# Graph network, last layer: one block for normalisation, weights, neighbours' products and the first sums

## The reference

```python
h = jnp.maximum(_layernorm(x, axis=-1), 0.0)
mask = (adj > 0).astype(x.dtype)
deg = jnp.sum(mask, axis=1, keepdims=True)
agg = mask @ h / jnp.maximum(deg, 1.0)
self_f = h @ W_self + b_self
nb_f = agg @ W_nb + b_nb
combined = jnp.concatenate([self_f, nb_f], axis=-1)
x = x + jax.nn.relu(combined @ W_comb + b_comb)
```

## Time and profile before

| | us |
|---|---|
| median of three runs | 2232.77 |
| the profiled execution, its own time | 2228.39 |
| its span, first to last instruction | 2226.7 |
| outside the span | 1.7 |
| the last layer, from the first DVE instruction of block one (2004.06) to the last output's DMA | 222.6 |
| of it: from 2004.06 to the first matmul of `sums(1)` (2065.77) | 61.7 |
| of it: from there to the end of the last matmul | 156.8 |

### The profile page before, as it was taken

One profiled execution on the slowest core, in us unless ns is written; L12 is line 12 of the kernel. 1 busy time (PEld: TensorE's weight loads), 2 busy tenths in 40 slices (PEclk: granted clock), 3 DMA queues, 4 the chain that ended last, 5 costly groups with the idle time before them and its releaser, 6 DMA issues. The chain is left out here.

```text
span 2226.7 us, 58732 instructions
## 1 busy us (share of the span) xinstructions
PE 1983.5 (89%) x23674; PEld 1553.7 (70%) x23674; DVE 1892.4 (85%) x4169; ACT 1614.1 (72%) x1924; POOL 926.3 (42%) x932
## 2 busy tenths in 40 slices
PE   5758999999986899999695999999999999886999
PEld 4548999999985788888553666666666666555544
DVE  5587999999997899987786999999999999985222
ACT  4557999999985776542444999999999999885100
POOL 0020000000006344454144888888888888860000
PEclk9958999999997899999796999999999999998999
DMA  9797211211201356778374122111121111101222
GB/s 313 293 360 291 98 67 56 99 65 63 95 12 41 85 136 154 165 169 175 70 159 134 61 70 70 70 54 53 70 70 70 65 41 70 39 2 53 81 81 70
DMA packets 173436, 233.32 MB, mean 105 GB/s; under 512 B 110113, under 2 KB 140865, under 8 KB 169839
## 3 DMA queue, kind: packets, MB, share of 16 engines
q1 hardware_dynamic: 148766, 201.87, 29.8%
q10 hardware_dynamic: 24400, 27.70, 3.8%
HBM read 156.67 MB, written 47.30 MB: 92 GB/s over the span
## 5 line engine op out<-in xcount | busy, mean ns | idle before, releaser
L1956 DVE CUSTOM_DVE_ANT_0 h_S<-h_ps,h_off 128x832 f32<-128x832 f32 x832 | 800.5, 1020 | 14.9 <-POOL h_off L1795 11.6
L1853 PE MATMUL h_ps<-KS,h_QS 98*128 98x416 f16 x1664 | 442.2, 348 | 80.2 <-DVE h_mx L1956 45.3
L1913 ACT ACTIVATE h_H<-h_S,h_nmx 128x2048 fp8e4<-128x2048 f32 x208 | 416.7, 2004 | 81.9 <-DVE h_nmx L1962 81.9
L844 ACT ACTIVATE b_CA<-room,HC 128x1152 fp8e4<-128x1152 f32 (+1 forms) x384 | 435.4, 1219 | 0.0
L945 PE MATMUL b_pb<-xb,room 128*128 128x132 f16 x5408 | 415.7, 222 | 3.8 <-DVE room L906 3.4
L945 PEld LDWEIGHTS b_pb<-xb,room 128*128 128x128 fp8e4 x5408 | 342.1, 97 | 6.4 <-DVE room L906 5.8
L1801 POOL TENSOR_SCALAR h_gap<-h_S,h_nmx 128x1280 f32<-128x1280 f32 x208 | 278.0, 1337 | 89.2 <-DVE h_nmx L1962 79.7
L1806 POOL TENSOR_SCALAR h_H<-h_gap 128x1280 uint8<-128x1280 f32 x208 | 260.8, 1254 | 17.2
L926 PE MATMUL b_pz<-xb,adjT 128*128 128x134 f16 x2704 | 257.8, 222 | 4.3 <-PEq L306 4.3
L1884 PEld LDWEIGHTS h_po<-Vhl,h_HT 128*128 128x128 fp8e4 x5408 | 214.9, 98 | 65.1 <-ACT h_HT L1920 0.7
L1853 PEld LDWEIGHTS h_ps<-KS,h_QS 98*128 98x128 f16 x1664 | 96.0, 97 | 198.6 <-DVE h_mx L1956 121.0
(11 more groups left out here) (227 smaller groups left out, 3226.0 us busy)
## 6 DMA issues: line engine op xcount, KB each, us to landing
h_rows<-in_adj_dram SPq DMA_DIRECT2D x25, 1663.5 KB, 7.6
room<-in_adj_dram SPq DMA_DIRECT2D x25, 832.0 KB, 7.1
room<-in_adj_dram SPq DMA_DIRECT2D x25, 831.5 KB, 8.0
e_dram<-c_U ACTq DMA_DIRECT2D x78, 256.0 KB, 3.1
xb<-xv_dram SPq DMA_DIRECT2D x44, 435.5 KB, 4.9
adjT_dram<-adjT SPq DMA_DIRECT2D x1, 10816.0 KB, 32.3
c_ad<-adjT_dram SPq DMA_DIRECT2D x13, 832.0 KB, 6.8
m_ad<-adjT_dram SPq DMA_DIRECT2D x13, 832.0 KB, 4.5
```

Of the source, the lines that this page charges most:

```text
L844: nc.scalar.activation(dst[:, 0:cols], elr[:, n % 2, 0:cols], ACT.Sigmoid, bias=HC[:, h, 1, jt:jt + 1], scale=STEP, saturate=False).then_i ...
L1853: last = nc.tensor.matmul(ps[:, ch % 2, b, 0:SB], QS[:, i % 2, h, :], KS[:, h, c0:c0 + SB], start=True, stop=True)
L1913: nc.scalar.activation(H[:, g % 2, 0:CA], S[:, g % 2, 0:CA], ACT.Exp, bias=nmx[:, g % 2:g % 2 + 1], scale=1.0, saturate=False).then_inc(s_ ...
L1956: nc.vector.tensor_tensor_reduce(out=two(S[:, g % 2, ch * SW:(ch + 1) * SW]), in0=ps[:, ch % 2, :, 0:SB], in1=two(off[:, i % 2, ch * SW:(c ...
```

## The change

`layer3` still runs two blocks. `mean_prepare` takes the place of `normalise` and `mean_weights`, and holds the neighbours' products of all 26 tiles and all of `sums(0)` as well. `mean_aggregate` keeps `own(0)` and everything from `sums(1)` on.

- **Statistics.** DVE begins with the mean and variance of tiles 0 to 3. The 1/deg operations go to the end of its list. There are four portions in place of two, and the chain of small operations is six long in place of seven.
- **Normalising.** The tiles are scaled and shifted without ReLU by POOL (20 tiles) and by ACT (the six of `BY_ACT`: 2, 3, 6, 7, 10 and 11). ReLU is applied after the transposes: by ACT in its copy of the high part, by DVE in that of the rest (`ALU.max`).
- **Transposes.** Two PSUM banks in place of four: `turn(g)` waits for DVE to have emptied the bank of `turn(g - 1)`.
- **Weights.** Each load has its own semaphore, the neighbours' matrix comes first, and the four bias columns and the bias row are issued behind the three matrices. One PSUM bank (`pm`) in place of two takes both joined matrices and then the bias row.
- **Neighbours' products** are copied out two tiles at a time (13 copies of 128x512 on ACT and on DVE in place of 26 of 128x256 on each).
- **First sums.** `first_sums(g)` follows two quads behind `neighbour(g)`. The first two chunks of the adjacency are loaded in the same block, behind the small loads.

The diff, cut to its core:

```diff
+def mean_prepare(k, ap, hT, m, bias, ideg, Pn, pa, ad, s_in, s_first, adjT_dram):
...
+    COUNTED = 7
+    BY_ACT = (2, 3, 6, 7, 10, 11)
+    RP = 3
...
+    SOURCES_IN = (1, 0)
...
+        pt = k.ps(c, "p3_pt", [P, KC, CH])
+        pp = k.ps(c, "p3_pp", [P, RP, CH])
+        pm = k.ps(c, "p3_pm", [P, CH])
...
+            for s in SOURCES_IN:
+                sp.dma_start(raw[:, s], srcs[s][0].rearrange("(k p) c -> p k c", p=P)).then_inc(s_raw[s], 16)
+            sp.dma_start(comb[:].rearrange("p s k c -> p (s k) c"),
+                         ap["L3_gnn_W_comb"].rearrange("(k p) c -> p k c", p=P)).then_inc(s_comb, 16)
+            for s in range(2):
+                for kc in range(KC):
+                    sp.dma_start(bcol[:, s, kc:kc + 1], srcs[s][1][kc * P:(kc + 1) * P].rearrange("(p o) -> p o", o=1)).then_inc(s_small, 16)
+            sp.dma_start(bc[:], ap["L3_gnn_b_comb"].unsqueeze(0).to_broadcast([P, D])).then_inc(s_small, 16)
+            for q in range(2):
+                sp.dma_start(ad[:, q].rearrange("p t j i -> p t (j i)").bitcast(U8),
+                             adjT_dram[q * CT:(q + 1) * CT].rearrange("t p n -> p t n").bitcast(U8)).then_inc(s_in[q], 16)
...
+            for t in [t for t in range(NT) if t not in BY_ACT]:
+                pool.wait_ge(s_sm, COUNTED * (portion_of(t) + 1))
+                nc.gpsimd.tensor_scalar(H[:, t, :], k.X[:, t, :], rt[:, t:t + 1], nb[:, t:t + 1], ALU.mult, ALU.add).then_inc(s_h, 1)
...
+                        ins = nc.vector.tensor_tensor(a, rs, rs, ALU.mult)
+                    elif n == 3:
+                        ins = nc.vector.scalar_tensor_tensor(b, a, -0.5 * HSC, ve, ALU.mult, ALU.mult)
+                    elif n == 4:
+                        ins = nc.vector.scalar_tensor_tensor(rt, b, 1.5 * HSC, rs, ALU.add, ALU.mult)
+                    else:
+                        ins = nc.vector.scalar_tensor_tensor(nb, mv[:, t0:t1, 0], -1.0, rt, ALU.mult, ALU.mult)
+                    ins.then_inc(s_sm, 1)
...
+            def low(g):
+                n0, n1 = cols(g)
+                for kc in range(KC):
+                    dve.wait_ge(s_hi, KC * g + kc + 1)
+                    nc.vector.scalar_tensor_tensor(hT[:, 1, kc, n0:n1], pt[:, kc, 0:n1 - n0], 0.0, hT[:, 0, kc, n0:n1],
+                                                   ALU.max, ALU.subtract).then_inc(s_lo, 1)
+
+            def neighbour_low(g):
+                for n in quad_pairs(g):
+                    dve.wait_ge(s_ph, n + 1)
+                    nc.vector.scalar_tensor_tensor(Pn[:, 2 * n:2 * n + 2, D:2 * D], pp[:, n % RP, :].rearrange("p (t d) -> p t d", t=2),
+                                                   AGSC / PSC, Pn[:, 2 * n:2 * n + 2, 0:D], ALU.mult, ALU.subtract).then_inc(s_pl, 1)
+
+            def weights_low(n):
+                s = SOURCES_IN[n]
+                dve.wait_ge(s_mhi, n + 1)
+                nc.vector.scalar_tensor_tensor(m[:, 1, s], pm[:].rearrange("p (k n) -> p k n", k=KC), WSC, m[:, 0, s],
+                                               ALU.mult, ALU.subtract).then_inc(s_mlo, 1)
...
+            measure(0, 4)
+            gather(0)
+            factors(0, 0, 1)
+            measure(4, 8)
+            factors(0, 1, COUNTED - 1)
+            measure(8, 12)
+            gather(1)
+            factors(1, 0, 1)
+            measure(12, 14)
+            factors(1, 1, COUNTED - 1)
+            measure(14, 20)
+            gather(2)
+            factors(2, 0, 1)
+            weights_low(0)
+            low(0)
+            factors(2, 1, COUNTED - 1)
+            measure(20, 23)
+            low(1)
+            weights_low(1)
+            measure(23, NT)
+            gather(3)
+            factors(3, 0, 1)
+            neighbour_low(0)
+            low(2)
+            factors(3, 1, COUNTED - 1)
+            neighbour_low(1)
+            low(3)
+            dve.wait_ge(s_small, 16 * SMALL)
+            nc.vector.tensor_copy(bb[:], bcol[:].unsqueeze(3).to_broadcast([P, 2, KC, P])).then_inc(s_bb, 1)
+            neighbour_low(2)
+            low(4)
+            neighbour_low(3)
+            low(5)
+            dve.wait_ge(s_b, 1)
+            nc.vector.tensor_tensor(bias[:], pm[:, 0:D], bc[:], ALU.add)
+            neighbour_low(4)
+            low(6)
+            neighbour_low(5)
+            nc.vector.tensor_scalar(dg[:, 0, :], k.deg[:], 1.0, None, ALU.max).then_inc(s_deg, 1)
+            dve.wait_ge(s_deg, 1)
+            nc.vector.reciprocal(dg[:, 1, :], dg[:, 0, :]).then_inc(s_deg, 1)
+            neighbour_low(6)
+            dve.wait_ge(s_deg, 2)
+            nc.vector.tensor_scalar(ideg[:], dg[:, 1, :], 1.0 / AGSC, None, ALU.mult)
+
...
+            def shifted(t):
+                act.wait_ge(s_sm, COUNTED * (portion_of(t) + 1))
+                nc.scalar.activation(H[:, t, :], k.X[:, t, :], ACT.Identity, scale=rt[:, t:t + 1], bias=nb[:, t:t + 1]).then_inc(s_ha, 1)
...
+            root(0)
+            shifted(2)
+            shifted(3)
+            for n, s in enumerate(SOURCES_IN):
+                act.wait_ge(s_tr, n + 1)
+                nc.scalar.activation(wt[:, s].rearrange("p k n -> p (k n)"), pp[:, n, :], ACT.Copy).then_inc(s_cp, 1)
+            root(1)
+            high(0)
+            for t in BY_ACT[2:]:
+                shifted(t)
+            weights_high(0)
+            root(2)
+            high(1)
+            weights_high(1)
+            neighbour_high(0)
+            high(2)
+            root(3)
+            neighbour_high(1)
+            for g in range(3, QUADS):
+                high(g)
+                neighbour_high(g - 1)
+            neighbour_high(QUADS - 1)
...
+            def turn(g):
+                pe.wait_ge(s_h, sum(t not in BY_ACT for t in range(quad(g)[-1] + 1)))
+                if quad(g)[-1] in BY_ACT:
+                    pe.wait_ge(s_ha, BY_ACT.index(quad(g)[-1]) + 1)
+                for kc in range(KC):
+                    if g:
+                        pe.wait_ge(s_lo, KC * (g - 1) + kc + 1)
+                    for n, t in enumerate(quad(g)):
+                        last = nc.tensor.transpose(pt[:, kc, n * P:(n + 1) * P], H[:, t, kc * P:(kc + 1) * P], k.ident[:])
+                    last.then_inc(s_ht, 1)
+
+            def neighbour(g):
+                pe.wait_ge(s_lo, KC * (g + 1))
+                for n in quad_pairs(g):
+                    if n >= RP:
+                        pe.wait_ge(s_pl, n - RP + 1)
+                    for e in range(2):
+                        t = 2 * n + e
+                        for x, (kc, a, b) in enumerate(prods):
+                            last = nc.tensor.matmul(pp[:, n % RP, e * D:(e + 1) * D], hT[:, a, kc, t * P:(t + 1) * P], m[:, b, 1, kc, :],
+                                                    start=(x == 0), stop=(x == len(prods) - 1), skip_group_check=True)
+                    last.then_inc(s_p, 1)
+
+            def first_sums(g):
+                if g == 0:
+                    pe.wait_ge(s_in[0], 16)
+                for n in quad_pairs(g):
+                    pe.wait_ge(s_pl, n + 1)
+                    for jt in (2 * n, 2 * n + 1):
+                        last = nc.tensor.matmul(pa[:, 0, :], ad[:, 0, 0, jt, :], Pn[:, jt, :], start=(jt == 0), stop=(jt == NT - 1))
+                if g == QUADS - 1:
+                    last.then_inc(s_first, 1)
+
+            for n, s in enumerate(SOURCES_IN):
+                pe.wait_ge(s_raw[s], 16)
+                for kc in range(KC):
+                    for kn in range(KC):
+                        last = nc.tensor.transpose(pp[:, n, kc * D + kn * P:kc * D + (kn + 1) * P],
+                                                   raw[:, s, kn, kc * P:(kc + 1) * P], k.ident[:])
+                last.then_inc(s_tr, 1)
+            def combine(n):
+                s = SOURCES_IN[n]
+                pe.wait_ge(s_cp, n + 1)
+                if n == 0:
+                    pe.wait_ge(s_comb, 16)
+                else:
+                    pe.wait_ge(s_mlo, n)
...
+            turn(0)
+            combine(0)
+            turn(1)
+            combine(1)
+            for g in range(QUADS):
+                if 1 <= g < QUADS - 1:
+                    turn(g + 1)
+                neighbour(g)
+                if g == 3:
+                    pe.wait_ge(s_bb, 1)
+                    pe.wait_ge(s_mlo, 2)
+                    for n, (s, kc) in enumerate([(s, kc) for s in range(2) for kc in range(KC)]):
+                        last = nc.tensor.matmul(pm[:, 0:D], bb[:, s, kc, :], comb[:, s, kc, :], start=(n == 0), stop=(n == 2 * KC - 1))
+                    last.then_inc(s_b, 1)
+                if g >= 2:
+                    first_sums(g - 2)
+            first_sums(QUADS - 2)
+            first_sums(QUADS - 1)
...
-                if c >= 2:
-                    sp.wait_ge(s_agg, CT * (c - 1))
+                sp.wait_ge(s_agg, CT * (c - 1) - 1)
...
-            for t in range(LEAD):
-                neighbour(t)
-            for i in range(NT):
```

(11 more changed lines are left out.)

179 lines of the change are left out of this document (84 added, 95 removed).

## The result

The changed kernel takes 2215.28 us, the median of four runs (2212.08 to 2218.97). Before, with one more run, it is 2232.72 us (2230.72 to 2234.2). The ratio is 0.9924, with a 95% interval of 0.9912 to 0.9936: 17 us less, with 14 to 20 as bounds. Forecast were 15.2 us less and 2217.6 us, which lies within these bounds: this result alone does not tell 17 from 15.

The account below looks back on a forecast made before the run. Block one was taken as bound by a weight load, then ACT; block two's first 22 us by PE. 2016.4 + 30.9 + 0.4 + 1.7 + 1.2 = 2050.6 in place of 2065.77: 15.2 us less, 2217.6 us, range 2212 to 2225.

Parts of the forecast that it names:

- Term 1: Start of the second quad's transposes, set by DVE's list: at 2016.4 us, bounds 2015.5 and 2019.
- Term 2: PE's work left from `turn(1)` to the end of the first sums: 30.9 us at high clock, plus 0.4 of gaps.
- the ring: PSUM loop of transposes, high part, rest, next transposes: hidden beside a quad's products, 3.5 us against 3.5; 0.4 added for gaps.
- rival 2: Last layer's block one: PSUM loop not hidden, quads' parts run in a row, 0.7 us of gain, 2232; chance 0.05.
- Term 3: PE's clock at `turn(1)`, low after a gap: half of 3.4 us, 1.7 added; bounds 0 and 3.4.
- if the clock falls again: Sign in the changed kernel's trace that would show the clock term, 1.7 us at `turn(1)`, to be wrong.
- Rival 4: PE finds its clock high at `turn(1)` and has no gaps: 17.3 us gained, 2215.5; within the forecast's 0.73.
- T: Time from DVE's first operation of the last layer to `sums(1)`'s first matmul: forecast 46.5 us in place of 61.7.
- Rival 3: PE stays at its low clock in block one and the kernel is slower; chance 0.05.
- Term 4: Crossing from block one to block two, with the last matmul's drain and `own(0)`: 1.2 us.
- Without them POOL would be last for `turn(1)`: Claim that without ACT's six tiles POOL would be last for `turn(1)`, by 4 x 0.54 us.
- Rival 1: DVE's small steps stretch beside POOL and PE idles between quads: gain 9.5 us, 2223.3; chance 0.17.

Follow-up runs that it names:

- The loads' experiment: Changed kernel with loads issued in before's order and PE waiting for all eight ahead of its first transpose: T 49.92 us, `turn(1)` at 17.75.
- the filled kernel: Changed kernel with 20 unread transposes into an unused PSUM bank between the first joined matrix and `turn(1)`: T 44.40 us, `turn(1)` at 12.24.
- the two executions with T at 44.4: Changed kernel with all 26 tiles shifted by POOL, T 44.42 us; and changed kernel with 20 unread transposes ahead of `turn(1)`, T 44.40 us.
- the second chip: Changed kernel once more, no edit, against before on that chip: 2214.34 us against 2234.6, ratio 0.9911, T 45.91 us.

## Why the prediction was right, point by point

**Term 1, the start of `turn(1)`: right to 0.1 us, with some luck.** 12.3 were forecast (2016.4 less 2004.06), 12.30 and 12.15 measured. The joined matrix came 0.42 us late for DVE, where I had added 0.2:

```profile
2021.17 0.69 DVE L2104 SCALAR_TENSOR_TENSOR m_w<-p_pm,m_w 128x512 f16<-128x512 f32 x1 [0.42 <-ACT m_w L2177]
```

Without that wait DVE's list took 11.7 us to the end of the first copy of `low(0)`, where 12.1 were summed, and another 0.15 us lie between that end and `turn(1)`. So a list 0.4 us too long in the sum made up for a wait 0.2 us too short and for those 0.15. The weights landed at 3.97 us in place of 2.9. How late the joined matrix comes depends on when the clock rises: where it rose at 8.2 us, DVE did not wait, and `turn(1)` started at 11.85. The loads' experiment shows that the tie between the two ways was real: PE's way later by 5.9 us moves `turn(1)` by 5.45.

**Term 2, the work behind it: right.** 30.9 us at the high clock were summed. From 2022.61 to the end of the last sum less its drain (0.16: one such matmul is 0.379 long in the changed kernel's trace, and they follow one another by 0.216), 2055.22, it is 32.6, of which 1.6 are the clock's: `turn(1)` 1.69 and the joined matrix 2.99, where the filled kernel has 1.16 and 1.89. The 0.4 us of small gaps were not needed; the ring is hidden, and rival 2 is out.

**Term 3, the clock: right size by luck, wrong mechanism.** I had the clock low at `turn(1)` because PE had been idle, and rising behind it. The 3.4 us that I halved stand in no row of before: the earlier trace rows, with PE's start at 2012.89, give 2.9; that half of such a stretch is lost was an estimate of mine. No run shows the term as I meant it: the first rise came 8.2 to 9.6 us after the layer's start (12.7 with the loads as before), ahead of `turn(1)` in every one. In the changed kernel the clock rose 9.2 us after the layer's start, during the first joined matrix and *before* `turn(1)` (12.3), and fell again in or behind the 2.1 us gap, to 0.50 from 12.6 to 16.0 us. The prediction's own sign against this term, "if the clock falls again", came true. Stretches of 2 us of the changed kernel:

```profile
2018.00:2020.00 2.00, 2.00 (x7) 1.59 (x7) 2.00 (x8) 2.00 (x5) 1.87 (x4) 0.63 1.03 386
2020.00:2022.00 2.00, 0.50 (x3) 0.10 (x1) 1.54 (x12) 1.24 (x4) 0.31 (x1) 1.00 0.59 231
2022.00:2024.00 2.00, 1.39 (x8) 1.36 (x9) 1.86 (x8) 0.52 (x1) 0.00 (x0) 0.72 0.10 40
2024.00:2026.00 2.00, 2.00 (x7) 1.62 (x6) 2.00 (x5) 0.68 (x2) 1.92 (x4) 0.50 0.00 0
2026.00:2028.00 2.00, 2.00 (x15) 1.64 (x14) 0.41 (x2) 0.60 (x1) 2.00 (x5) 0.92 0.00 0
```

That is 3.4 us at a granted clock of 0.50. It cost 1.6 us by the filled kernel, and the sum had 1.7. Rival 4 (the clock up at `turn(1)`) is what the two executions with T at 44.4 had. Rival 3 is out: only 3.4 us of PE's 32.6 ran low.

**Term 4, the crossing: right.** 1.14 us from 2055.22 to 2056.36, and 1.2 forecast.

**T of before was the weak step.** All of the sum was set against 61.7 us as if that were a property of the kernel. It scatters by 4 us, and the sum had nothing for it but half of 4.4 us in the range, without a reason. The measured time lies 2.3 us below the forecast, which is within the interval of the measured gain (14 to 20 us); on the second chip, with 20 us (16 to 24), it is not. T itself was forecast at 46.5 and measured at 46.05 and 45.91. That the layers ahead take 2.5 to 6.5 us longer stands in no term at all, and it hid part of the scatter: that the forecast of the whole time is so near owes something to luck.

**The six tiles on ACT.** "Without them POOL would be last for `turn(1)`" is wrong: POOL's four tiles end at 10.3 us at the latest, DVE's rest at 12.2. I had the 2.2 us and did not set them beside the date at which `turn(1)` could start. What the six tiles do is another thing, up to 0.4 us: with them POOL is idle while DVE makes its small steps.

**Rival 1** is out in this kernel: the ten small steps took 0.16 to 0.20 us each, since POOL was idle during both chains (until 2014.49, and from 2015.59 to 2018.13), as read. Where the two do meet, the rows show the price. With POOL shifting all tiles:

```profile
2013.08 0.62 DVE L2064 BATCH_NORM_AGGREGATE p_mv<-p_stats 128x2 f32<-128x6 f32 x8
2013.74 0.43 DVE L2075 TENSOR_SCALAR p_sm<-p_mv 128x8 f32<-128x8 f32 x1
```

The second of these took 0.43 us next to POOL's tiles of 2011.97 to 2014.14, and 0.17 in the changed kernel. What holds the step up beside them, no run here shows.

## What to carry to other kernels

When stages of one engine's work are merged into one list, the gain is the waiting between them, and it is read from a stretch's busy time, not from the work moved: 9.5 of 15.7 us here were overlap (6.5 of them waiting), and where the moved sums stood in the list was worth 1.3. Find the one instruction from which the bound engine runs dense, and count what stands ahead of it on the queue that releases it, down to the statistics of tiles that nobody needs yet; but the next bound is near: of 2.85 us by which `turn(1)` came earlier, new gaps took 1.3. Small loads issued between large ones, with the engine waiting for all, cost 3.9 to 5.5 us here, for four loads of 0.5 KB, one of 128 KB and a matrix that was not needed yet; most of it is the waiting for all, and the order at most 1 us. A stretch in which the clock falls and rises should be profiled two or three times before a change is set against it: before's took 61.7, 63.4 and 65.6 us.
